# Query and key terms placed by DMA through DRAM, routing interleaved with the first strips, and two value buffers

## The reference

```python
xn = layernorm(x)                          # [2048, 256]
q, k, v = split(xn @ Wqkv.T)               # 16 heads of 16
q, k = rope(q), rope(k)
attn = softmax(causal(q @ k.T * 16**-0.5)) @ v @ Wout.T
c = gate(xn)        # 32 experts; groups of 4, best 4 of 8 groups, then 6 experts a token
y = sum_e c[:, e] * ((silu(xn @ w11[e].T) * (xn @ w33[e].T)) @ w22[e].T)
shared = (silu(xn @ sw1.T) * (xn @ sw3.T)) @ sw2.T
out = x + attn + y + shared
```

## Time and profile before

| | |
|---|---|
| median of 3 runs | 957.71 us (954.71 to 959.66) |
| the profiled execution | 964.53 us, span 962.6 us |
| busy, share of span | PE 90%, DVE 65%, POOL 55%, ACT 53% |
| projections | up to about 111 us |
| first strip of attention | 145.5 us |
| experts | about 421 to 640 us |

### The profile page before, as it was taken

How to read it: one execution, slowest core, us unless ns; L and a number is a source line. 1 busy time by engine, 2 the same in 40 slices (tenths; PEclk the granted TensorE clock), 3 DMA queues, 4 the chain that set the end, 5 groups by cost and what they waited for, 6 DMA issues and landing times.

```text
span 962.6 us, 18240 instructions
## 1 busy us (share of the span) xinstructions
PE 869.7 (90%) x5601; PEld 478.6 (50%) x5602; DVE 622.8 (65%) x1271; ACT 511.2 (53%) x1222; POOL 527.5 (55%) x712
## 2 busy tenths in 40 slices
PE   5799766798989987989999999989999999999997
PEld 2366443333343432468878887753444344443344
DVE  2688936788856776755555555546688857978422
ACT  3444251255666564634445444447666677666662
POOL 2033339958979316056666666528886887830000
PEclk9899985799999999999999999989999999999998
DMA  7001002000000001037787786945552452520011
GB/s 208 1 11 39 25 4 66 1 1 2 1 2 1 2 1 50 1 106 241 218 242 227 230 244 182 126 106 72 73 72 33 58 73 31 72 34 1 9 37 45
DMA packets 55932, 70.93 MB, mean 74 GB/s; under 512 B 11552, under 2 KB 47392, under 8 KB 55840
## 3 DMA queue, kind: packets, MB, share of 16 engines
q0 software_dynamic: 19968, 31.47, 18.4%
q1 hardware_dynamic: 18976, 21.53, 7.4%
q10 hardware_dynamic: 16896, 16.78, 5.2%
HBM read 48.53 MB, written 21.23 MB: 72 GB/s over the span
## 4 chain that ended last, share of the span: by engine, by line
PE 43%; issue 40%; DVE 7%; ACT 3%; DMA 3%; SPq 2%; DVEq 1%; ACTq 0%
PE bank L1126 9%; PE bank L1111 7%; PE vector_banks L1091 6%; PE vector_banks L1191 5%; PE vector_banks L982 4%; PE vector_banks L1001 4%; DVE mpart L896 4%; PE bank L1001 2%; PE bank L1204 2%; DMA xn_all<-wexp 2%; PE vector_banks L1146 2%; ACT turned L571 2%; PE bank L982 2%; SPq L414 1%; PE bank L1017 1%
## 5 line engine op out<-in xcount | busy, mean ns | idle before, releaser
L660 ACT ACTIVATE probs<-bank 128x512 f32<-128x512 f32 (+3 forms) x640 | 313.4, 536 | 226.6 <-PE bank L1114 104.8
L896 DVE TENSOR_REDUCE mpart<-vector_banks 128x2 f32<-128x1024 f32 (+3 forms) x320 | 327.0, 1062 | 98.2 <-PE vector_banks L1091 60.4
L1111 PE MATMUL bank<-turned 99*128 99x512 bf16 (+3 forms) x640 | 208.9, 358 | 16.2 <-ACT probs L660 8.5
L1091 PE MATMUL vector_banks<-turned 96*128 96x512 bf16 (+3 forms) x640 | 185.9, 362 | 16.9 <-DVE mpart L896 12.9
L539 POOL DMA_INDIRECT turned<-normed_rows,tok_i x128 | 125.5, 981 | 96.0 <-PE vector_banks L982 79.1
L554 POOL DMA_INDIRECT res<-expert_rows,slot_i x96 | 148.5, 1547 | 41.3 <-issue 29.9
L1126 PE MATMUL bank<-probs,V 128*32 128x512 f32 (+3 forms) x1280 | 152.9, 548 | 1.7 <-ACT probs L660 1.3
L1111 PEld LDWEIGHTS bank<-turned 99*128 99x128 bf16 x640 | 58.9, 98 | 183.5 <-ACT probs L660 111.9
L1191 PE MATMUL vector_banks<-xn_all,probs 128*128 x512 | 135.4, 387 | 4.6 <-issue 2.0
L1191 PEld LDWEIGHTS vector_banks<-xn_all,probs 128*128 128x128 f32 x512 | 87.1, 190 | 17.3 <-issue 9.2
L571 ACT ACTIVATE probs<-bank 128x128 f32<-128x128 f32 (+1 forms) x256 | 83.9, 330 | 18.1 <-PE bank L1204 4.3
(11 more groups left out here) (154 smaller groups left out, 1001.9 us busy)
## 6 DMA issues: line engine op xcount, KB each, us to landing
expert_rows<-probs ACTq DMA_DIRECT2D x32, 512.0 KB
xn_all<-wexp SPq DMA_DIRECT2D x32, 384.0 KB
normed_rows<-xn_all SPq DMA_DIRECT2D x4, 512.0 KB, 3.2
turned<-normed_rows,tok_i POOLq DMA_INDIRECT x128
out<-res SPq DMA_DIRECT2D x16, 128.0 KB, 1.7
res<-x SPq DMA_DIRECT2D x1, 1536.0 KB, 9.4
res<-expert_rows,slot_i POOLq DMA_INDIRECT x96
probs<-wqkvT SPq DMA_DIRECT2D x1, 768.0 KB, 5.3
```

Source lines behind the costliest of these rows:

```text
L660: A(PT[v // 2 % 4][:, v % 2, 0:width], bank[A_BANK[step][0]][:, 0:width], ACT.Exp).then_inc(s["scalar_bank_read"], 1)
L896: V.tensor_reduce(mpart[:, t % TPC, 2 * j:2 * j + 2, p], ring[:, :, 0:w], AX.X, ALU.max).then_inc(s["vector_bank_read"], 1)
L1091: last = mm(ring[:, h, 0:w], q_turned(slice(0, KQ), 2 * j + h, t * P, P), k_turned(par, slice(0, KQ), 2 * j + h, p * CH, w), start=True, s ...
L1111: last = mm(ring[:, 0:CH - off], k_turned(parity(g), slice(0, KM), h, kb * P, P), q_turned(slice(0, KM), h, c * CH + off, CH - off), start ...
```

## The change

- **Terms for all groups at once.** During the projections GpSimd splits each tile of queries and keys once, into three parts (`split`). TensorE turns these (`turn_terms`, 12 transposes a tile), ScalarE copies them to `staged`. Every four tiles SyncE stores each part to each of the places it takes, into a DRAM tensor `term_rows`, and loads the rows of a group and chunk from there into `turned` (`load_terms`). `prepare`, `cat_q`, `cat_k` and the steps `q` and `k` are gone, in all groups.
- **Attention begins at the projections' end.** The routing of the last quarter, counts, ranks and slots become steps `route`, `counts`, `ranks`, `owner`, `slots`: one behind each of the first eight strips, then two at a time. The terms of the last two tiles are turned behind the opening. Buffers move so that the first part of `turned` is free during the projections.
- **Two value buffers.** `V4` is a list of two; the step `v4` comes after chunk 2 of the group before.
- `TOKENS_FROM, TOKENS_TO` go from 7, 48 to 8, 50.

```diff
-    order = [step for c in range(NCH) for step in turns(0, c)]
+    chain = [("route", i) for i in range(ROUTE_PIECES)]
+    chain += [("counts",), ("slots", 0), ("ranks",)] + [("slots", i) for i in range(1, 7)]
+    chain += [("owner",)] + [("slots", i) for i in range(7, SLOT_PIECES)]
+    order = []
+    for step in strips(0, 0):
+        order += [step, chain.pop(0)]
     opening = len(order)
...
+        for _ in range(2):
+            if chain:
+                order.append(chain.pop(0))
...
-            if pending[1] == NCH - 1:
+            if pending[1] == NCH - 2 and pending[0] + 1 < NG:
                 order.append(("v4", pending[0] + 1))
...
     sync:
+            def load_terms(kind, g, c):
+                at, arrived = (0, q_in[c]) if kind == 0 else ((1 + parity(g)) * HG * T, k_in[parity(g)][c])
+                sp.dma_start(QK[0:KQ, at:at + HG * T].rearrange("p (h q) -> p h q", q=T)[:, :, c * CH:(c + 1) * CH],
+                             term_rows[kind, g * HG:(g + 1) * HG, :, :, c * CH:(c + 1) * CH].rearrange("h s d t -> (s d) h t")
+                             ).then_inc(arrived, 16)
...
             for quarter in range(4):
...
+                sp.wait_ge(s["terms_read"], 2 * QT4 * (quarter + 1))
+                for kind in range(2):
+                    for place, n in enumerate(SLOT_TERM[kind]):
+                        for half in range(2):
+                            sp.dma_start(term_rows[kind, half * H // 2:(half + 1) * H // 2, place, :, quarter * CH:(quarter + 1) * CH],
+                                         staged[quarter % 2][:, n, 2 * kind + half, :]).then_inc(s["terms_stored"], 16)
+                sp.wait_ge(s["terms_stored"], 16 * STORES * (quarter + 1))
+                for kind in range(2):
+                    load_terms(kind, 0, quarter)
...
     gpsimd:
+            for t in range(NT):
+                b = t % 2
+                gp.wait_ge(s["qk_ready"], t + 1)
+                if t >= 2:
+                    gp.wait_ge(s["terms_turned"], 2 * (t - 1))
+                gp.tensor_copy(split[b][:, 0, :], qk[b][:, :])
+                gp.drain()
+                gp.tensor_tensor(left[:, :], qk[b][:, :], split[b][:, 0, :], ALU.subtract)
+                gp.drain()
+                gp.tensor_copy(split[b][:, 1, :], left[:, :])
+                gp.drain()
+                gp.tensor_tensor(split[b][:, 2, :], left[:, :], split[b][:, 1, :], ALU.subtract).then_inc(s["terms_made"], 1)
...
     scalar:
+            def terms_turned(t, kind):
+                act.wait_ge(s["terms_turned"], 2 * t + (1 if kind else 2))
+                if t >= 2 * QT4:
+                    act.wait_ge(s["terms_stored"], 16 * STORES * (t // QT4 - 1))
+                copy(staged[t // QT4 % 2][:, :, 2 * kind:2 * kind + 2, t % QT4 * P:(t % QT4 + 1) * P],
+                     term_bank(t, kind)).then_inc(s["terms_read"], 1)
...
     tensor:
+            def turn_terms(t, kind):
+                pe.wait_ge(s["terms_made"], t + 1)
...
+                for n in range(SPLIT):
+                    for a in range(2):
+                        last = turn(term_bank(t, kind)[:, n, a, :], split[t % 2][:, n, (2 * kind + a) * P:(2 * kind + a + 1) * P],
+                                    identb[:, :])
+                last.then_inc(s["terms_turned"], 1)
```

More of the change, by code:

```diff
@@ L172, in whole_order @@
     some(True)
-    assert not later
+    assert not later and not chain
     order += [("pv", *pending), ("oe", *pending[:2]), ("ot", *pending[:2])]
@@ L268, in layer @@
         xn_all = sb("xn_all", [P, NT, D])
-        qk_all = sb("qk_all", [P, NT, 2 * D])
+        qk = [at_first([P, 2 * D]) for b in range(2)]
+        split = [at_first([P, SPLIT, 2 * D], BF16) for b in range(2)]
+        left = at_first([P, 2 * D])
+        staged = [at_first([P, SPLIT, COLS, CH], BF16) for b in range(2)]
         v_all = sb("v_all", [P, NT, D])
@@ L427, in _ @@
                 load(b, b, True)
+            for c in range(NCH):
+                used(0, c)
+                load_terms(0, 1, c)
+            for c in range(NCH):
+                load_terms(1, 2, c)
+            for c in range(NCH - 1):
+                used(1, c)
+                load_terms(0, 2, c)
             with sp.Fori(1, E // NB) as i:
@@ L430, in _ @@
                     load(NB * i + b, b)
+            used(1, NCH - 1)
+            load_terms(0, 2, NCH - 1)
+            for c in range(NCH):
+                load_terms(1, 3, c)
+            for c in range(NCH):
+                used(2, c)
+                load_terms(0, 3, c)
             for t in range(NT):
@@ L498, in _ @@
-            for quarter in range(4):
-                gp.wait_ge(s["qk_ready"], QT4 * (quarter + 1))
-                prepare(0, slice(QT4 * quarter, QT4 * (quarter + 1)), quarter % 2 == 1)
-            def prepare_next(g, half):
-                for ring, full in ((A_AT, "scalar_bank_full"), (D_AT, "vector_bank_full")):
-                    read = [ring[step] for c in (2 * half, 2 * half + 1) for step in turns(g - 1, c) if step in ring]
-                    if read:
-                        gp.wait_ge(s[full], max(read) + 1)
-                prepare(g, slice(HALF * half, HALF * (half + 1)))
@@ L635, in attend @@
                     n = A_AT.get(step)
-                    if step[0] in ("q", "k") and n is not None:
-                        kind, g, j, c = step
-                        at, rows = (0, KQ) if kind == "q" else ((1 + parity(g)) * HG * T, KM)
-                        act.wait_ge(s["scalar_bank_full"], n + 1)
-                        copy(two_heads(at, slice(0, rows), j, c),
-                             bank[A_BANK[step][0]][0:rows, :].bitcast(BF16).rearrange("p (h q) -> p h q", q=CH)
-                             ).then_inc(s["scalar_bank_read"], 1)
-                    elif step[0] == "pv":
+                    if step[0] == "pv":
                         pvs += 1
@@ L897, in attend @@
                                         ALU.max).then_inc(s["vector_bank_read"], 1)
-                    elif step[0] == "k" and n is not None:
-                        _, g, j, c = step
-                        dve.wait_ge(s["vector_bank_full"], n + 1)
-                        V.tensor_copy(two_heads((1 + parity(g)) * HG * T, slice(0, KM), j, c),
-                                      ring[0:KM, 0, :].bitcast(BF16).rearrange("p (h q) -> p h q", q=CH)
-                                      ).then_inc(s["vector_bank_read"], 1)
+                    elif step[0] == "route":
+                        next(routing_steps, None)
+                    elif step[0] == "slots":
+                        next(slot_steps, None)
                     elif step[0] == "mc":
@@ L944, in attend @@
                         V.tensor_copy(tok_i[:, :], gu_bank[:, 0:SLOT_TILES]).then_inc(s["tok_ready"], 1)
-            dve.wait_ge(s["weights_stored"], 16 * 4)
+            attend(opening)
+            shared_add(NT - 1)
             attend(early)
+            assert next(routing_steps, "over") == "over" and next(slot_steps, "over") == "over"
             def rows(n):
```

325 lines of the change are left out of this document (179 added, 146 removed).

## The result

The changed kernel takes 923.01 us, median of 4 runs (921.92 to 924.36), against 957.79 for the kernel before beside it: ratio 0.964, 95% interval 0.961 to 0.967. Run again on another chip it was 918.70 against 953.64, ratio 0.967 (0.963 to 0.972). The forecast was 921, 904 to 943.

The account below looks back on a forecast made before the run. TensorE was taken to set the pace in projections and attention, with a serial passage between. Terms +10.4 - 27.9 + 3.8 + 8 - 28.8 - 2 = -36.5 from 957.7 gave 921 us, range 904 to 943.

Parts of the forecast that it names:

- the signs: Projections ending at 120 to 124, first strip 126 to 130, first score 144 to 148, experts some 16 us earlier, lasting as long.
- Projections, +10.4: Projections: 12 added transposes a tile cost +8.9 us on full TensorE, plus +1.5 for bank 0; end at 121.7.
- Bank 0's term: Projections: terms in bank 0 must be read before the next row is turned into it; +1.5 us, bounds 0 and +6.
- VectorE and GpSimd blocking each other: Rival, projections: GpSimd and two-input VectorE instructions stop each other, 7.5 us a routing tile, +14, so 935; chance 0.11.
- Opening and first chunk, +3.8 and +8: First strip to first score: route steps between strips, +3.8 us; first chunk: rest of the chain, +8, bounds +3 and +15.
- Attention, -28.8: Attention, groups 1 to 3: 48 turn steps go, each priced near TensorE's own time, 0.6 us.
- The rival with dearer turns: Rival, attention: turns held score banks, transposes and copy in series 1.67 us; up to -16 further, 905; chance 0.15.
- Values, -2: Group boundaries: ScalarE's copy of values moves a chunk ahead, three boundaries at 0.7 us; bounds 0 and -3.2.
- DMA, nothing: Stores and loads of terms: 12 us issuing and 19 us transfer a quarter, under the 25.6 of four tiles; no cost.
- The rival had them from 1.32 us a store upward: Rival: stores do not keep up, stalls at tiles 8 and 12; 7 us at 1.32 a store, 980 at 2.4; chance 0.05.
- Cheaper turns: Rival, attention: turns cost less than TensorE's own time; half price and chain at +11 give -19, so 939; chance 0.14.
- no effect: Rival: passage is short but its work only sits in the first chunk, at +15 and clock below 0.74: 928.

Follow-up runs that it names:

- the first profile: The kernel before, unchanged, in its first profiled execution: 964.5 us (span 962.6), 6.8 above the median of its runs.
- the two second profiles: The kernel before and the changed kernel, both unchanged, each profiled once more: spans 953.4 and 915.6 us.
- the pieces: Changed kernel with GpSimd's fill of the ones rows cut into 8 pieces between term tiles 2 to 9: 915.67 us, ratio 0.960 to the kernel before.
- the run that moved it out: Changed kernel with the router's steps ahead of the first chunk's strips and the slot-placing steps behind them: 927.60 us, ratio 0.974 to the kernel before.

## Why the prediction was right, and where it was not

The time was right (923 against 921), the sum -34.8 against -36.5. Its terms were not all so; errors of +6 (a fill), +4 (the base) and -8 us (the turns) nearly cancelled, and that is luck. What was right is the account of where the time goes: TensorE's added work in the projections, the chain's in the first chunk, and the turns as the gain in attention. Of the signs, the experts came 17 us earlier than in the first profile (12 between the two second profiles; forecast 16) and lasted as long. First strip and first score came late, for the reason given under the fills.

*Projections, +10.4.* They ended at 128.4. Without the late start (next term) that is 122.2, against 121.7 forecast. TensorE stayed full, 6.5 us a tile against 6.4, and doubling the transposes cost 6 to 8 us more, a little under the 8.9 of the sum. Bank 0's term wasn't measured by itself; the two together were right.

*A term that was missing: the fills.* The sum had nothing for the two new fills on GpSimd. The first delays the start by 6.2 us, all of it on the path: the pieces gave 5.8 back. It also explains why first strip (134.75) and second chunk (188.1 against 181.9 forecast) both came 6 to 7 us late. The prediction did look at VectorE and GpSimd blocking each other, but only in the projections, and put 4 to 6 us of GpSimd work per tile against it. There VectorE's operations got longer (the two-input one of L784 from 0.44 to 0.72 us, but also a one-input `TENSOR_SCALAR` of 128x128 from 0.27 to 0.85), 10 us over 13 tiles where the sum left VectorE's time as it was. TensorE stayed full all the same. What hurt was one long instruction where nothing hides. The Trainium skill, in SBUF — State Buffer, section "SBUF: two separate sides", states the shared port pair as a lock for the whole instruction, taken by any GpSimd operation and by VectorE operations in a two-port mode, while two-input ones only contend with GpSimd work that reads SBUF. The trace agrees: `TENSOR_SCALAR` stood for 6.20 us behind a fill that reads nothing, `TENSOR_TENSOR` ran in 0.16 beside it. In which mode `TENSOR_SCALAR` ran no row shows. The prediction quoted only the half of the rule on two inputs, and that was the wrong half for a fill.

*Opening and first chunk, +3.8 and +8.* From first strip to first score it is 18.3 us (forecast 17.7), with 1.6 in the second fill; from there to the second chunk 35.1 (forecast 36.3). Both right, and the chain's share of the chunk was 7.3 by the run that moved it out. But the base was not: in the first profile of before, the first chunk ran at a clock of 0.74, in the second at 0.83 and 2.8 us shorter. That makes the change 3 to 4 us worse up to the second chunk than the one profile tells.

*Attention, -28.8, the step that was mis-sized.* 48 turns took 37.4 us when put back, 0.78 each and not 0.6, and the profiles' 38.7 agree. The sum priced a turn at near TensorE's own time, and that is the wrong mechanism: this part costs 0.19. The rival with dearer turns (up to 44.8) was as near in size, but not for its reason: it had the held bank and the copy in series. Taken away one at a time, the copies' time is worth some 4 us of 37 and the wait for them about 1.5 (less than the 3 us that the times tell apart); TensorE's transposes by themselves cost 9 to 10. The other 60% come with turns being steps of their own in the score order. At a chunk's start no strip runs for 7.6 us, and over seven chunks TensorE's idle is 12 us with the turns as steps, 4.8 with their transposes slipped in and 9.3 without them; how the one leads to the other is argued and not shown. The argument that TensorE's idle caps what a turn can cost beyond its own time was not sound either, though its 28 us were not passed. It counted transposes at their full time, while they lie partly in gaps when placed ahead of a strip's products. And a share of 95% busy did not mean that TensorE's work could not be packed closer: the same matmuls had 226.3 us of busy time in one order and 231.0 in another.

*Values, -2.* Nothing measurable. ScalarE is busy 61 to 68% in attention; that its spare time is the reason was not tested.

*DMA, nothing.* Right. From the first store to the loads it is 0.81 us a store against 0.8 forecast (issuing alone is 0.66, forecast 0.51). The reserve is real but finite: with double the stores the two stalls appear at tiles 8 and 12. The rival had them from 1.32 us a store upward, where it counted one stall of 7 us; 48 stores in 31.25 us are 1.3 per wanted store, and gave stalls of 8 and 16, so that the rival's reckoning was too mild. It left out the time from the end of the last issue until ScalarE could read into the buffer, 4.9 and 5.9 us, and the loads behind it, so that the next quarter's stores begin only at 100.72 where the last issue ended at 93.96.

*The other rivals.* Cheaper turns and no effect are out: turns put back cost 0.78 each, and the span shrank. GpSimd's work blocking VectorE's cost 6 us, at the start, not 14 in the projections.

## What to carry to other kernels

Work that moves to a loader or to an idle engine has set-up instructions of its own (fills, ones, clears). Price each with its place in the timeline: ask which engine's next instruction it can hold, and cut it in pieces behind something that hides it. And what a small step costs in a tight interleave isn't its instructions' time: here 8 transposes cost 0.19 us slipped in before a matmul that takes its bank anyway, and 0.7 or more as a step with its own place, bank and copy. Before a sum is made against one profile, profile once more: here the first chunk alone differed by 2.8 us.

## What the runs showed of the hardware

- A GpSimd fill of 3 partitions x 8192 bf16 values took 6.92 us, 0.84 ns a value along the free dimension, on three partitions; pieces of 512 words of 4 bytes took 0.52 each (4.2 for the same bytes).
- A VectorE `TENSOR_SCALAR` of 128x4 values (0.17 us when alone) lasted 6.20 us behind that fill, and one of 128x16 lasted 1.77 behind a fill of 1.81; `RECIPROCAL` (0.18) and `TENSOR_TENSOR` (0.16) beside the first fill took what they take without it (0.18 and 0.16 in the kernel with the ones in pieces).
- In 13 tiles of the projections, with GpSimd busy 47.4 of 85.3 us where it had been 21.7 of 74.8, a VectorE `TENSOR_SCALAR` of 128x128 took 0.85 us on average (0.27 before) and a two-input operation of 128x256 took 0.72 (0.44 before). Which of GpSimd's instructions they stood behind was not read.
